# Three split passes for three of the eight key tiles of the attention's last product

## The reference

```python
# layer 0: depthwise 3x3 convolution to 3C, 1x1 to 2C, gelu, 1x1 to C, residual
perceived = conv_general_dilated(x, w_perc, ..., feature_group_count=Cc) + b_perc
x_new = x + w_up2(gelu(w_up1(perceived)))
# then attention of each pixel over its 3x3 neighbours, residual
return h_new + _local_attn(h_new, w_qkv, b_qkv)
# layer 1: group norm, attention of all 1024 pixels over all 1024, projection, residual
xn = group_norm(x, gamma, beta)
q, k, v = xf @ Wq + bq, xf @ Wk + bk, xf @ Wv + bv
attn = softmax(einsum('bnc,bmc->bnm', q, k) * scale)
out = einsum('bnm,bmc->bnc', attn, v) @ Wp + bp
return xn + out
```

## Time and profile before

| what | us |
|---|---|
| median of 3 runs | 1000.25 (999.46 to 1000.75) |
| the profiled execution | 1000.03 |
| its span, first to last instruction | 998.2 |
| PE busy | 954.1 |
| DVE busy | 789.8 |
| ACT busy | 613.8 |
| POOL busy | 357.6 |

### The profile page before, as it was taken

How to read it: one execution, slowest core, us unless ns; L and a number is a source line. 1 busy time by engine, 2 the same in 40 slices (tenths; PEclk the granted TensorE clock), 3 DMA queues, 4 the chain that set the end, 5 groups by cost and what they waited for, 6 DMA issues and landing times. The chain is left out here.

```text
span 998.2 us, 18592 instructions
## 1 busy us (share of the span) xinstructions
PE 954.1 (96%) x5572; PEld 850.5 (85%) x5572; DVE 789.8 (79%) x1594; ACT 613.8 (61%) x1252; POOL 357.6 (36%) x334
## 2 busy tenths in 40 slices
PE   4988999999999999999999999999999999999877
PEld 3876989889898988989898898989889898988766
DVE  6775978878787887978788797878879787898862
ACT  2565765757466675746667574666757466677432
POOL 3625244351523425152342515234251523431101
PEclk9997999999999999999999999999999999999989
DMA  5100663745566363656737465673746567357663
GB/s 97 22 1 1 191 180 117 190 130 189 137 197 181 116 189 123 192 137 196 182 116 189 123 192 137 196 182 116 189 123 192 137 195 181 118 169 222 193 208 95
DMA packets 170305, 150.71 MB, mean 151 GB/s; under 512 B 71584, under 2 KB 154016, under 8 KB 170272
## 3 DMA queue, kind: packets, MB, share of 16 engines
q1 hardware_dynamic: 169424, 149.90, 52.5%
q10 hardware_dynamic: 848, 0.39, 0.2%
HBM read 75.82 MB, written 74.45 MB: 151 GB/s over the span
## 5 line engine op out<-in xcount | busy, mean ns | idle before, releaser
L688 PE MATMUL work<-et,vv_t 128*128 128x256 f32 x1024 | 233.2, 381 | 0.0
L688 PEld LDWEIGHTS work<-et,vv_t 128*128 128x128 f32 x1024 | 192.1, 190 | 26.2
L1422 POOL TENSOR_TENSOR g_lo<-u,g_hi 128x512 fp32r<-128x512 f32 x60 | 76.4, 1284 | 303.0 <-ACT g_hi L987 303.0
L521 PE MATMUL work<-t_lo,wc_hi 128*128 128x256 f32 x576 | 170.3, 296 | 9.3 <-DVE wc_lo L1667 7.2
L1851 DVE STREAM_TRANSPOSE et<-e_by_keys 128x1024 f32<-128x1024 f32 x126 | 155.5, 1235 | 9.5 <-DMA e_by_keys<-e_blocks 8.8
L523 PE MATMUL work<-t_hi,wc_hi 128*128 128x256 f32 x576 | 162.8, 283 | 0.0
L522 PE MATMUL work<-t_hi,wc_lo 128*128 128x256 f32 x576 | 162.4, 282 | 0.0
L521 PEld LDWEIGHTS work<-t_lo,wc_hi 128*128 128x128 f32 x576 | 109.7, 190 | 11.4 <-issue 7.8
L522 PEld LDWEIGHTS work<-t_hi,wc_lo 128*128 128x128 f32 x576 | 109.9, 191 | 0.7
L523 PEld LDWEIGHTS work<-t_hi,wc_hi 128*128 128x128 f32 x576 | 109.3, 190 | 0.0
L1073 ACT ACTIVATE e<-ps_t,nm 128x1024 f32<-128x1024 f32 x63 | 70.2, 1114 | 47.3 <-DVE et L1851 36.1
(11 more groups left out here) (185 smaller groups left out, 2288.9 us busy)
## 6 DMA issues: line engine op xcount, KB each, us to landing
e_blocks<-e SPq DMA_DIRECT2D x126, 512.0 KB, 3.2
e_by_keys<-e_blocks SPq DMA_DIRECT2D x126, 512.0 KB, 4.5
x_in<-in_x SPq DMA_DIRECT2D x64, 128.0 KB, 5.1
out<-r_tok SPq DMA_DIRECT2D x32, 256.0 KB, 3.6
w_up_t<-in_L_conv_w_up SPq DMA_DIRECT2D x1, 384.0 KB, 4.3
const<-in_const ACTq DMA_DIRECT2D x1, 166.0 KB, 5.1
y<-in_L_conv_w_up ACTq DMA_DIRECT2D x1, 128.0 KB, 5.0
y<-in_L_conv_w_qkv SPq DMA_DIRECT2D x1, 128.0 KB, 4.5
```

The costliest lines, as they stand in the source:

```text
L521: te.matmul(dst, wh, xl, start=first, stop=False)
L688: mm = te.matmul(bank("pv", j, n)[:, 0:256], vv_t[:, kt, :], et[:, kt, pixels_], start=kt == 0, stop=kt == TILES - 1)
L1422: return pool.tensor_tensor(dst, full, hi, ALU.subtract)
```

## The change

`SPLIT = 3`: in `values`, key tiles 0 to 4 are multiplied as before, tiles 5 to 7 through `mm3`. For these, `et_hi_tile` (ACT) rounds 128 x 384 of each `et_turn` into `et_hi`, a buffer for two pairs of query tiles, and `et_lo_tile` (POOL) writes the difference over `et`; `vv_half(n, 1)` also writes `vv_hi`, and `vv_lo_part` (DVE) writes `vv_lo`. The second bank of `vv` is free only after `vv_lo_part`. The programs of all engines and the three bank plans are in a new order; of these the turns stand below, as far as the order around these steps goes. The rest of the work is the same.

Buffers, and what frees the bank of `vv`:

```diff
+SPLIT = 3
...
-        et = placed("et", [128, TILES, PIX], et_at)
+        et, et_lo = placed("et", [128, TILES, PIX], et_at), placed("et_lo", [128, TILES, PIX], et_at, F32R)
+        et_hi = sb("et_hi", [128, SPLIT, HALF], F32R)
+        vv_hi, vv_lo = (sb(f"vv_{p}", [128, SPLIT, 128], F32R) for p in ("hi", "lo"))
...
+            if x == 1 and u == "vv":
+                return vv_lo_ready.after(n, 0)
```

SP's turn:

```diff
                 move_out(a, 3)
+                load_x(d)
                 move_in(a, 2)
...
                 move_in(a, 5)
-                load_x(d)
                 move_out(a, 7)
+                store(a, 0)
                 move_in(a, 6)
                 move_in(a, 7)
-                store(a, 0)
                 store(a, 1)
```

PE, `values` and the second half of its turn:

```diff
-                for kt in range(TILES):
-                    mm = te.matmul(bank("pv", j, n)[:, 0:256], vv_t[:, kt, :], et[:, kt, pixels_],
-                                   start=kt == 0, stop=kt == TILES - 1)
+                for kt in range(TILES - SPLIT):
+                    te.matmul(bank("pv", j, n)[:, 0:256], vv_t[:, kt, :], et[:, kt, pixels_], start=kt == 0, stop=False)
+                te.wait_ge(*et_lo_ready.after(n, 2 * j + 1))
+                te.wait_ge(*vv_lo_ready.after(n, 0))
+                for k in range(SPLIT):
+                    mm = mm3(bank("pv", j, n)[:, 0:256], (vv_hi[:, k, :], vv_lo[:, k, :]),
+                             (et_hi[:, k, (j % 2) * 256:(j % 2 + 1) * 256], et_lo[:, TILES - SPLIT + k, pixels_]),
+                             False, k == SPLIT - 1)
                 mm.then_inc(pe["pv"].handle, 1)
...
                 local_probs_t(b, 3)
+                scores(a, 6)
                 local_values(b, 0)
-                scores(a, 6)
+                scores(a, 7)
                 local_values(b, 1)
                 values(a, 0)
-                scores(a, 7)
+                group_moments(b)
                 up2(c, 0)
-                group_moments(b)
                 values(a, 1)
-                k(c, 0)
                 v(c, 0)
+                output_projection(a, 0)
+                up2(c, 1)
+                kk(b, 0)
                 qq(b, 0)
-                output_projection(a, 0)
-                kk(b, 0)
-                values(a, 2)
-                up2(c, 1)
-                kk(b, 1)
                 q(c, 0)
                 qq(b, 1)
+                k(c, 0)
+                kk(b, 1)
+                values(a, 2)
+                scores(b, 0)
+                k(c, 1)
                 v(c, 1)
-                scores(b, 0)
+                q(c, 1)
+                values(a, 3)
                 vv(b, 0)
-                k(c, 1)
-                values(a, 3)
-                q(c, 1)
                 vv(b, 1)
                 output_projection(a, 1)
```

ACT; of the eight `et_hi_tile` of its turn three stand ahead of `exp(a, 5)`, and `exp(a, 3)` has moved ahead of `take(c, 2, 3)`:

```diff
+                if k == 1:
+                    act.activation(vv_hi[:, :, :], bank("vv", 1, n)[:, (4 - SPLIT) * 128:].rearrange("p (t c) -> p t c", t=SPLIT),
+                                   ACT.Copy)
...
+            def et_hi_tile(n, t):
+                act.wait_ge(*et_ready.after(n, t))
+                if t % 2 == 0:
+                    act.wait_ge(*pe["pv"].after(n, t // 2 - 2))
+                act.activation(et_hi[:, :, (t % 4) * 128:(t % 4 + 1) * 128], et[:, TILES - SPLIT:, t * 128:(t + 1) * 128],
+                               ACT.Copy).then_inc(et_hi_ready.handle, 1)
```

POOL, the step and its turn:

```diff
+            def et_lo_tile(n, t):
+                cols_ = slice(t * 128, (t + 1) * 128)
+                pool.wait_ge(*et_hi_ready.after(n, t))
+                minus(et_lo[:, TILES - SPLIT:, cols_], et[:, TILES - SPLIT:, cols_],
+                      et_hi[:, :, (t % 4) * 128:(t % 4 + 1) * 128].bitcast(F32)).then_inc(et_lo_ready.handle, 1)
...
-                residual(a, 0)
+                et_lo_tile(a, 0)
+                et_lo_tile(a, 1)
+                et_lo_tile(a, 2)
                 g_lo_part(c, 0)
                 g_lo_part(c, 1)
                 inverse_deviation(b)
-                h_lo_half(c, 0)
-                xn_lo_half(b, 0)
+                et_lo_tile(a, 3)
                 g_lo_part(c, 2)
                 g_lo_part(c, 3)
+                residual(a, 0)
+                xn_lo_half(b, 0)
+                h_lo_half(c, 0)
                 xn_lo_half(b, 1)
+                et_lo_tile(a, 4)
+                et_lo_tile(a, 5)
                 h_lo_half(c, 1)
+                differences(d)
+                et_lo_tile(a, 6)
+                et_lo_tile(a, 7)
+                transform(d)
                 residual(a, 1)
-                differences(d)
-                transform(d)
```

DVE; in the turn `vv_lo_part(b)` is the last call, and `group_variance(b)` follows `channel_moments(b)` at once:

```diff
+            def vv_lo_part(n):
+                dve.wait_ge(*vv_ready.after(n, 1))
+                dve.tensor_tensor(vv_lo[:, :, :], bank("vv", 1, n)[:, (4 - SPLIT) * 128:].rearrange("p (t c) -> p t c", t=SPLIT),
+                                  vv_hi[:, :, :].bitcast(F32), ALU.subtract).then_inc(vv_lo_ready.handle, 1)
```

More of the change, by code:

```diff
@@ L431, in fill_program @@
                 load_x(3)
+                store(0, 0)
                 move_out(0, 7)
@@ L481, in drain_program @@
                 move_out(B - 2, 2)
+                store(B - 3, 0)
                 move_in(B - 2, 1)
@@ L788, in fill_program @@
                 group_moments(1)
-                scores(0, 7)
                 up2(2, 0)
                 values(0, 1)
+                v(2, 0)
+                output_projection(0, 0)
+                up2(2, 1)
                 kk(1, 0)
+                kk(1, 1)
+                v(2, 1)
                 qq(1, 0)
+                q(2, 0)
+                k(2, 0)
                 qq(1, 1)
                 values(0, 2)
[L796 to L801, removed]
+                k(2, 1)
                 scores(1, 0)
-                v(2, 1)
+                q(2, 1)
+                values(0, 3)
                 vv(1, 0)
-                values(0, 3)
-                k(2, 1)
-                q(2, 1)
                 vv(1, 1)
@@ L869, in drain_program @@
                 local_probs_t(B - 2, 0)
+                conv(B - 1, 1)
                 conv(B - 1, 2)
+                local_probs_t(B - 2, 1)
+                scores(B - 3, 4)
                 conv(B - 1, 3)
-                scores(B - 3, 4)
-                local_probs_t(B - 2, 1)
                 scores(B - 3, 5)
@@ L876, in drain_program @@
                 conv(B - 1, 4)
+                conv(B - 1, 5)
+                local_probs_t(B - 2, 3)
                 local_values(B - 2, 0)
-                local_probs_t(B - 2, 3)
                 scores(B - 3, 6)
-                conv(B - 1, 5)
                 local_values(B - 2, 1)
-                scores(B - 3, 7)
                 values(B - 3, 0)
@@ L902, in drain_program @@
                 local_scores(B - 1, 1)
+                values(B - 3, 2)
                 local_scores(B - 1, 2)
+                v(B - 1, 0)
                 scores(B - 2, 3)
-                values(B - 3, 2)
-                local_scores(B - 1, 3)
                 local_probs_t(B - 1, 0)
@@ L1151, in fill_program @@
                 wc_hi_unit(4)
+                take(0, 0, 1)
+                t_hi_part(0, 1)
+                wc_hi_unit(5)
+                take(0, 2, 3)
                 t_hi_part(0, 2)
-                take(0, 2, 3)
-                wc_hi_unit(5)
+                w0_hi_part()
+                w1_hi_part()
+                w2_hi_part()
                 t_hi_part(1, 0)
                 w_vp_part()
+                t_hi_part(1, 1)
+                take(1, 0, 1)
                 gelu(0, 0)
@@ L1270, in turn_program @@
                 local_exp(b, 0)
+                local_scale(b, 0)
                 take(c, 0, 1)
+                exp(a, 2)
                 local_exp(b, 1)
-                exp(a, 2)
-                local_scale(b, 0)
-                pt_pair(b, 0)
                 local_exp(b, 2)
                 local_scale(b, 1)
+                exp(a, 3)
+                local_exp(b, 3)
+                pt_pair(b, 0)
+                et_hi_tile(a, 0)
                 take(c, 2, 3)
-                exp(a, 3)
@@ L1280, in turn_program @@
                 local_scale(b, 2)
                 pt_pair(b, 1)
[L1282 removed]
+                local_scale(b, 3)
                 exp(a, 4)
[L1284 removed]
+                et_hi_tile(a, 1)
                 pt_pair(b, 2)
+                et_hi_tile(a, 2)
+                pt_pair(b, 3)
                 exp(a, 5)
[L1287 removed]
                 gelu(c, 0)
                 gelu(c, 1)
+                gelu(c, 2)
                 g_hi_part(c, 0)
[L1291 removed]
+                g_hi_part(c, 1)
@@ L1301, in turn_program @@
+                h_hi_half(c, 0)
+                exp(a, 7)
+                kk_hi_half(b, 0)
+                qq_hi_half(b, 0)
+                q_half(c, 0)
+                et_hi_tile(a, 5)
+                h_hi_half(c, 1)
                 k_half(c, 0)
-                exp(a, 7)
-                qq_hi_half(b, 0)
-                kk_hi_half(b, 0)
-                xn_hi_half(b, 1)
+                qq_hi_half(b, 1)
```

(35 more changed lines are left out.)

598 lines of the change are left out of this document (328 added, 270 removed), and 54 rows, old and new, of tables (BANK_PLAN, DRAIN_PLAN, FILL_PLAN).

## The result

The changed kernel takes 1005.21 us (median of 15 runs, 1001.34 to 1010.39); the kernel before, in the same comparison, 999.47 us (15 runs, 997.68 to 1000.86). The ratio is 1.0058, with a 95% interval from 1.0047 to 1.0068: slower by 0.6%, where 985 us and "faster" were forecast, and outside the range of 973 to 997. The profiled execution is the longest of these, 1010.39 us with a span of 1008.6.

A forecast was written before the change was run, and what follows sets the result against it. PE was taken to bound the loop, busy 57.8 of 58.2 us a turn. From about 1000 us: -14.8 products, -2.7 `xn_lo` wait, +1.2 new waits, +1.5 end, giving 985 us; range 973 to 997.

The forecast's parts named there:

- The term -14.8: PE's `values` products: three tiles at 354 instead of 431 ns save 231 ns per `values`, 14.8 us in 64.
- The `xn_lo` wait: PE's recurring loop wait of 5.4 us in all: a gain of 0 to 5.4 us, taken as 2.7.
- New waits, "0.1 us a turn": Allowance for added or moved waits in the loop: 0.1 us a turn, 1.2 us in 12 turns.
- `values(a,3)`, "hidden, by 2.4 us": Chain through store(a,0), move_in, et_turn, et_hi and et_lo takes 12.3 us, covered by 14.7 us of PE work.
- The bank of `vv(1)` and `up2(c,0)`: Bank free some 2.5 us into the turn, wanted at 3.5, hidden; up2(c,0)'s `g_lo` ends 1.2 us before it is needed.
- The end: Drain: the last `values` wait for `et_hi` and `et_lo` copies, 0 to 3 us, taken as 1.5 us more.
- The filling: New orders of filling and draining: change in PE's idle time taken as 0, with 5 us to either side.
- Rival 1: POOL's `et_lo` slows DVE to 56.9 us a turn, level with PE; half the gain gone, 993 us; chance 0.15.
- Rival 2: The x load ahead of move_in(a,2) on SP delays it and stops PE each turn: slower, 1013 us; chance 0.11.
- Rival 3: All new waits hidden, three passes at three quarters of fp32's price: 975.4 us; chance 0.05, shared with a shorter filling.
- Rival 4: No change: ACT's or POOL's queue holds PE back by just the 1.4 us gained a turn, 999 us; chance 0.04.

The follow-up runs named there:

- e2: Kernel before, own order, three key tiles multiplied in three passes from constant zero tiles, no added steps on other engines: 991.1 us, ratio 0.9915.
- e3: Changed kernel with a_part(a,1) put ahead of xn_hi_half(b,1) in ACT's turn: 994.57 us, ratio 0.9946.
- e6: e3 plus, on DVE, transform_two(d) moved behind et_turn(a,7): 993.66 us, ratio 0.9928.
- e5: e3 plus, in ACT's drain, a_part(B-2,3) moved right behind exp(B-1,3): 992.87 us, ratio 0.9916.
- e4: Changed kernel with output_projection(a,0) behind up2(c,1) on PE, output(a,0) behind h_half(c,1) on DVE, their banks exchanged: 1001.3 us, ratio 1.0035.
- e7: Changed kernel without POOL's et_lo_tile, products reading et_hi in its place, so part of the result is left out: 998.27 us, ratio 0.9997.
- e9: e1 with the edit of e3, a_part(a,1) ahead of xn_hi_half(b,1) on ACT: 997.21 us, ratio 0.9983.
- e10: Kernel before, own order and bank plan, with the split's products and steps put in right behind what each needs: 1051.53 us, ratio 1.0533.
- e1: Changed kernel's order with all eight key tiles in plain fp32, without et_hi, et_lo, vv_hi and vv_lo: 1007.15 us, ratio 1.0069.
- e8: Changed kernel with the edits of e3, e5 and e6 together: 993.83 us, ratio 0.9938.

## Why the prediction was wrong

The chip's answer was slower by 0.6%; forecast was faster by 1.5%. Point by point:

- **The price of the products was right, its yield was not.** Records at 216 ns and passes at 118 ns, nothing added by the change of form, 0.92 us less work a turn. The step that failed is "a microsecond less of PE work in a turn is a microsecond of the turn": e2 shows 0.66 of 0.92 in a turn and, outside the eleven turns, 0.6 of 4.6 us (filling and rest of e2). The term -14.8 should have been about -8. Two reasons could be read before: the wait for `xn_lo` in the earlier trace rows means that part of the turn hangs on a chain outside PE, and shorter products don't shorten that; and PE's 13.7 idle microseconds in the drain mean the same there.
- **The `xn_lo` wait** went down by 4.4 us, from 5.4 to 1.0; -2.7 was taken, within 0 to 5.4. Mechanism and size were right, at the good end; in e3, where PE no longer stands for `a_all` ahead of it, the wait doesn't come back.
- **New waits, "0.1 us a turn": the step that turned the sign.** They are 1.03 us for `a_all`, 0.43 around `values(a,3)` and some 0.4 of small ones, 1.9 us a turn in place of 0.1, and 22 us in twelve turns in place of 1.2. The bullet on `xn_lo` counts the projection that moved ahead of `kk` and `qq` as 0.9 us of cover, but not what that projection needs itself: `a_part(a,1)`, queued on ACT behind `xn_hi_half(b,1)`. The list of moved steps asked who waits for what is behind; it didn't ask of the moved consumer where its producer stands. The rows of before would have told: `a_part(a,1)` began 4.1 us after the first product of `values(a,1)` (541.76 to 545.85), and the new PE order comes for it after `values`, 3.2, and `v`, 0.9, the same 4.1, though the projection can't start before `a_part` ends. No rival of mine held this.
- **`values(a,3)`, "hidden, by 2.4 us"**: not quite. The wait isn't for `et_lo`, which never stops PE within `values`, but for `et_turn(a,7)` ahead of the plain tiles, so those 2.2 us are no cover for it. In e6 the wait goes when `transform_two(d)`, whose halves each took about 1.0 to 1.4 us in a turn, no longer stands ahead.
- **The bank of `vv(1)` and `up2(c,0)`** were hidden as said; no wait of theirs recurs.
- **The end**: +1.5 was taken, and -3.5 for the 15 `values` of the rest. The rest of the span is 3.9 us longer (165.3 to 169.2), of which 1.3 are that its first turn is still a turn of the loop with its waits (58.4 against 57.1); what the lower clock has of the other 2.6 (0.96 against 0.98) isn't shown. In e3 it is 0.6 longer, and e5 shows why nothing is gained: the wait changes its place.
- **The filling** is 3.3 us longer in the profiled execution, within the 5 allowed. The same order of the filling is 0.7 us longer in e3 and 2.7 shorter in e4, so no cost of this order is shown (more below).
- **Rival 1** (DVE drawn level by POOL) is true in kind: DVE grew by 3 us a turn beside 0.55 of new work, and e7 prices it at 0.44 us a turn. POOL's added work isn't the cause of the main wait. But work of POOL that the new order moved has a part in it: beside two `g_lo` the group norm's pair takes 2.17 us, before 1.37 (last section). An estimate from the rows of ACT and DVE above: with 0.53 us for each of the pair, ACT would come to `a_part(a,1)` some 0.6 us earlier, and 0.4 of the 1.03 us would be left. No run moved the `g_lo` away; e3 and e9 show that with `a_part` ahead the late group norm no longer stops PE there.
- **Rival 2** (the x load) didn't happen: no gap ahead of `up2(c,0)`, and `exp` waits for `et_turn` less than before, 29.6 us in all against 39.7. **Rival 3** falls with the 118 ns. **Rival 4** came nearest in kind, a queue of ACT that holds PE back, but I gave it 4% and no place.

In sum for the profiled execution: eleven turns +3.3 where about -11 was expected (0.92 + 0.2 - 0.1 a turn), filling +3.3 where -1 was (five `values`), the rest +3.9 where -2 was.

## What to carry to other kernels

When the order of an in-order queue is rewritten, follow each moved consumer back to its producer's new place in that producer's own queue, and do it for every step that moves ahead; a step counted as cover for another wait must itself be ready. Price a saving on the busiest engine by the stretch: where a wait recurs on it, a part of the saving goes into that wait, and where it drains, all of it may. Idle time of an engine is not by itself room for a step: in e10 half of POOL's turn and a third of ACT's are idle, and the turn is still 2.8 us longer than before. That a step whose input is late holds up what is queued behind it is the likely reason; no run separates it.

## What the runs showed of the hardware

**A DVE operation with one tile as its input is held up by POOL as well.** The group norm (L1823 before, L1932 after) reads one tile and per-partition scalars. Its groups (count, busy us, mean ns):

```profile
L1823 DVE TENSOR_SCALAR y<-y,gn 128x512 f32<-128x512 f32 x32 | 21.3, 706 | 0.6
```

```profile
L1932 DVE TENSOR_SCALAR y<-y,gn 128x512 f32<-128x512 f32 x32 | 32.7, 1062 | 0.6
```

Before, POOL stood waiting for `xn_hi` for much of that time (its 1.03 us in the earlier trace rows): 18 of the 32 had none of its tensor operations beside them and took 0.53 to 0.55 us each; the other 14 began beside one (`h_lo` in 13 cases) and took 0.92 to 0.94. After, two `g_lo` and a residual run there:

```profile
490.41 2.71 POOL L1485 TENSOR_TENSOR g_lo<-u,g_hi 128x512 fp32r<-128x512 f32 x2
493.08 1.45 POOL L1545 TENSOR_TENSOR r_tok<-vv_t,bp_row 128x512 f32<-128x512 f32 x1
```

The pair of that moment ends at 493.40, 0.28 us after the two `g_lo` (493.12). So does each of the 29 operations of the changed kernel, and of the 14 before, beside which one of POOL's ended: 0.28 to 0.29 us after that end, up to 1.52 us long. In e1, which has this order and no `et_lo`, the mean is 1062 ns too, in e7 1080, in e2, which has the old order, 714: it is the moved `g_lo`, not the new work, that does it. The prediction named the Trainium skill (SBUF — State Buffer, SBUF: two separate sides) for operations with two SBUF inputs; the same sentence has the lock also for a DVE operation in a 2-port performance mode, and by that rule, the trace agrees (706 against 1062 ns); that this operation runs in such a mode no run here shows.

**The filling has three lengths for one order.** The changed kernel, e3, e4, e5, e6 and e8 have the same filling. Its third `group_moments` comes at 189.1 us in e4, at 192.4 to 193.0 in e3, e5 and e6, at 195.1 in the changed kernel and at 196.0 in e8. The window from 30 to 40 us, of e3 and then of e8, with the granted clock before the last two columns:

```profile
30.00:40.00 10.00, 9.55 (x80) 9.35 (x80) 7.40 (x10) 3.48 (x10) 7.72 (x9) 1.00 0.21 28
```

```profile
30.00:40.00 10.00, 10.00 (x58) 10.00 (x59) 4.99 (x6) 1.77 (x5) 5.08 (x6) 0.63 0.32 41
```

In e8 most of this stretch ran at the lower clock level of 1.2 GHz, and PE did 58 records in place of 80. The changed kernel's profiled execution is like e8 (0.65), the one of before like e3 (1.00). e4 is like e3 here, and keeps 1.00 from 70 to 80 us, where e3 has 0.66. Ahead of it PE waits some 6 us for `wc_lo` in each of them, and the products after that begin 0.8 us apart (23.62 us in e3, 24.45 in e8); what decides isn't settled. The times go with it: of the changed kernel's 15 executions the five with a mean granted clock of 0.992 or more took 1001.34 to 1004.23 us, the ten with 0.989 or less 1004.79 to 1010.39; of e3's ten, three took 990.47 to 991.45 and seven 993.77 to 997.45, parted in the same way. In which stretch an execution without a trace lost its time isn't shown.
